# Causal attention on one core: a new order of the steps on each engine, row maxima taken 27 chunks ahead, and their split and the copy of the values on GpSimd

## What is computed

```python
scores = jnp.einsum('bhqd,bhkd->bhqk', Q, K) / np.sqrt(D_HEAD)
causal = jnp.triu(jnp.full((t, t), -jnp.inf, dtype=scores.dtype), k=1)
attn = jax.nn.softmax(scores + causal, axis=-1)
O = jnp.einsum('bhqk,bhkd->bhqd', attn, V)
```

## Time and profile before

| | |
|---|---|
| median of three runs | 861.2 us |
| the profiled execution | 859.2 us, span 857.6 us |
| TensorE busy | 739.3 us, 86% |
| VectorE busy | 683.2 us, 80% |
| ScalarE busy | 567.2 us, 66% |
| GpSimd busy | 423.4 us, 49% |
| attention | 61.5 to 549.8 us |

### The profile page before, as it was taken

The page is one execution under the profiler, slowest core; times in us unless marked ns, Lnnn a source line. Parts: engine busy times, 40 slices in busy tenths (PEclk is TensorE's granted clock), DMA queues, the critical chain, the costliest instruction groups (busy, mean ns, idle before and its releaser), DMA issues. The chain is left out here.

```text
span 857.6 us, 17568 instructions
## 1 busy us (share of the span) xinstructions
PE 739.3 (86%) x4345; PEld 323.0 (38%) x4345; DVE 683.2 (80%) x2289; ACT 567.2 (66%) x926; POOL 423.4 (49%) x468
## 2 busy tenths in 40 slices
PE   6758999999999999999999998696788888887755
PEld 4432233333332333233323331243456555554345
DVE  5669999898988898898889881156788888888883
ACT  4440267666766676667666767558889797897881
POOL 8655112221222112211222122267899999999984
PEclk9875699999999999999999999987999999999997
DMA  6757535335533653364336331201001101100000
GB/s 174 226 152 198 114 71 132 76 93 116 128 76 84 125 120 75 81 137 116 86 74 137 82 68 33 90 2 52 1 0 38 38 1 37 38 1 13 1 14 25
DMA packets 58955, 67.06 MB, mean 78 GB/s; under 512 B 15488, under 2 KB 33536, under 8 KB 58880
## 3 DMA queue, kind: packets, MB, share of 16 engines
q1 hardware_dynamic: 53120, 62.35, 30.5%
q10 hardware_dynamic: 5184, 2.36, 1.0%
q0 software_dynamic: 576, 1.57, 0.7%
HBM read 46.73 MB, written 19.53 MB: 77 GB/s over the span
## 5 line engine op out<-in xcount | busy, mean ns | idle before, releaser
L697 ACT ACTIVATE probs<-ps 128x384 f32<-128x384 f32 (+2 forms) x384 | 291.9, 810 | 174.4 <-PE ps L751 123.4
L668 POOL TENSOR_SCALAR_AFFINE_SELECT probs<-probs 128x256 f32<-128x256 f32 x256 | 102.9, 407 | 368.6 <-ACT probs L697 366.3
L807 DVE CUSTOM_DVE_ANT_0 junk<-ps,tri 128x256 bf16<-128x256 f32 (+3 forms) x512 | 229.1, 488 | 43.7 <-PE ps L719 36.0
L719 PE MATMUL ps<-Kx,Qx 128*128 128x512 bf16 (+3 forms) x768 | 230.8, 345 | 11.3 <-DVE mx L811 4.1
L751 PE MATMUL ps<-Qa,Ka 128*128 128x512 bf16 (+3 forms) x768 | 185.9, 328 | 15.0 <-DMA Qa<-m_scr 10.1
L737 PE MATMUL ps<-probs,Vg 128*9 128x512 f32 (+3 forms) x1536 | 159.3, 488 | 1.0 <-ACT Os L682 0.5
L811 DVE TENSOR_REDUCE mx<-ps 128x1 f32<-128x512 f32 x256 | 158.2, 679 | 0.3 <-DVE Vg L794 0.2
L719 PEld LDWEIGHTS ps<-Kx,Qx 128*128 128x128 bf16 x768 | 68.7, 97 | 204.4 <-DVE mx L807 124.8
L966 POOL TENSOR_TENSOR S<-sim 128x1024 f32<-128x1024 f32 x64 | 120.6, 1907 | 12.1 <-DVE A L1218 6.5
L1218 DVE SCALAR_TENSOR_TENSOR A<-S,T,ps 128x511 f32<-128x511 f32 x128 | 90.2, 741 | 11.3 <-ACT ps L1040 10.3
L751 PEld LDWEIGHTS ps<-Qa,Ka 128*128 128x128 bf16 x768 | 61.5, 97 | 90.8 <-ACT probs L697 44.3
(11 more groups left out here) (115 smaller groups left out, 868.5 us busy)
## 6 DMA issues: line engine op xcount, KB each, us to landing
Qx<-q_scr SPq DMA_DIRECT2D x48, 192.0 KB
Kx<-k_scr SPq DMA_DIRECT2D x48, 192.0 KB
Qa<-q_scr SPq DMA_DIRECT2D x48, 192.0 KB
Ka<-k_scr SPq DMA_DIRECT2D x48, 192.0 KB
o_scr<-Os SPq DMA_DIRECT2D x32, 256.0 KB, 2.1
q_scr<-qs SPq DMA_DIRECT2D x34, 128.0 KB, 3.3
k_scr<-qs SPq DMA_DIRECT2D x18, 128.0 KB, 3.3
xin<-in_L_attn_x_dram ACTq DMA_DIRECT2D x8, 256.0 KB, 3.7
```

Of the source, the lines that this page charges most:

```text
L668: pool.affine_select(out=diag, in_=diag, compare_op=ALU.is_ge, fill=0.0, base=0, pattern=[[0, 2], [1, P]], channel_multiplier=-1).then_inc ...
L697: act.activation(probs[:, k % 2, hh, 0:width], ps[:, bank:bank + 2, :].rearrange("p a c -> p (a c)")[:, 0:width], ACT.Exp, scale=SM_SCALE) ...
L719: pe.matmul(ps[:, X_BANK + f % X_SLOTS, 0:c1 - c0], Qx[:, u, hh, P * i:P * (i + 1)], Kx[:, u, hh, c0:c1], start=True, stop=True).then_inc( ...
L807: dve.tensor_tensor_reduce(out=junk[:, f % 4, 0:w], in0=src, in1=tri[:, CHUNK - w:CHUNK], scale=1.0, scalar=-BIG, op0=ALU.add, op1=ALU.max ...
```

## The change

1. `AHEAD` goes from 20 to 27, and `GROUP_ORDER` has a new order of the same 48 x, 24 s and 12 p.
2. The split leaves VectorE except for its first step (`row_max`) and the turn (`turn_max`), which now comes four chunks later (`TURN_LATER`). In between GpSimd does five steps: the three arithmetic ones, the cast, and a negation of its own into a new tile `mneg`.
3. The copy of the values into `Vg` goes from VectorE to GpSimd.
4. On GpSimd both stand between the masks of unit 1 and those of unit 4.
5. In SyncE's queue the store of an output's second half goes behind the next group's loads of `Qa` and `Ka`, and the store of the first half goes behind the maxima's write and loads.

```diff
-AHEAD = 20
+AHEAD = 27
+TURN_LATER = 4
-GROUP_ORDER = "psxxxpxxsxxsxsxpxspxxsxxpxxxspxxssxxsxpxsxxxsxpxxxsxspsxxsxpxxsxsxxsxpxxsxpxsxsxsxsx"
+GROUP_ORDER = "pxxpsxxsxxxsxxspxpsxsxxpxsxxpxsxsxxsxxxspxsxpxsxsxpxsxxsxpxxsxsxpxsxxsxpxsxsxxsxsxx"
...
                         load_parts(sp, Qa[:, 1 - u], Ka[:, 1 - u], bass.ds(n + 1, 1), sop_loaded[1 - u])
-                        store_o(n, 0)
+                        if not isinstance(n, int) or n > 0:
+                            store_o(n - 1, 1)
                         if ahead:
                             load_next_max(n + 3, 1 - u)
                         m_rows(n + 1, 1 - u, bass.ds(n + 1, 1))
-                        store_o(n, 1)
+                        store_o(n, 0)
...
+                    def split_max(g):
+
+                        c = M_STEPS * g
+                        wait_alone(pool, m_chain, c + 1, pads_made)
+                        pool.tensor_scalar(mneg[:], mm_[:], -1.0, 0.0, ALU.mult, ALU.add)
+                        wait_alone(pool, m_stored, 16 * g, pads_made)
+                        pool.tensor_scalar(msp[:, 0:32], mm_[:], -1.0, 0.0, ALU.mult, ALU.add).then_inc(m_chain, 1)
+                        wait_alone(pool, m_chain, c + 2, pads_made)
+                        pool.tensor_tensor(mr[:], mneg[:], msp[:, 0:32], ALU.subtract).then_inc(m_chain, 1)
+                        wait_alone(pool, m_chain, c + 3, pads_made)
+                        pool.tensor_copy(msp[:, 32:64], mr[:]).then_inc(m_chain, 1)
+                        wait_alone(pool, m_chain, c + 4, pads_made)
+                        pool.tensor_tensor(msp[:, 64:96], mr[:], msp[:, 32:64], ALU.subtract).then_inc(m_chain, 1)
...
+                    def group(n, u, last):
+                        masks(n, DIAG_UNITS[:2])
+                        if not last:
+                            wait_alone(pool, pv_done, PPG * n + PV_START, pads_made)
+                            pool.tensor_copy(Vg[:, 1 - u, :, :, :], vaug[:, bass.ds(n + 1, 1), :, :, :].rearrange(
+                                "p n j h d -> p (n j) h d")).then_inc(v_staged, 1)
+                            split_max(n + 1)
+                        masks(n, DIAG_UNITS[2:])
...
                             if f + AHEAD == CPG - 1 and last < 2:
-                                split_max(n + 1)
+                                row_max(n + 1)
+                            if f + AHEAD == CPG - 1 + TURN_LATER and last < 2:
+                                turn_max(n + 1)
```

More of the change, by code:

```diff
@@ L68 @@
 CPG = len(MAXC)
-AHEAD = 20
-GROUP_ORDER = "psxxxpxxsxxsxsxpxspxxsxxpxxxspxxssxxsxpxsxxxsxpxxxsxspsxxsxpxxsxsxxsxpxxsxpxsxsxsxsx"
+AHEAD = 27
+TURN_LATER = 4
+GROUP_ORDER = "pxxpsxxsxxxsxxspxpsxsxxpxsxxpxsxsxxxsxxxspxsxpxsxsxpxsxxsxpxxsxsxpxsxxsxpxsxsxxsxsxx"
 CARRIED = 4
@@ L576, in build @@
             mm_ = sa("rowmax", [P, 32])
+            mneg = sa("mneg", [P, 32])
             mr = sa("mr", [P, 32])
@@ L626, in group @@
                         m_rows(n + 1, 1 - u, bass.ds(n + 1, 1))
-                        store_o(n, 1)
+                        store_o(n, 0)
                     load_next_max(2, 0)
-                    with sp.Fori(0, GROUPS // 2 - 2) as i:
+                    group(0, 0, True)
+                    group(1, 1, True)
+                    with sp.Fori(1, GROUPS // 2 - 2) as i:
                         for u in range(2):
@@ L635, in _ @@
                     group(GROUPS - 2, 0, False)
+                    store_o(GROUPS - 2, 1)
                     for half in range(2):
@@ L660, in _, with masks @@
                     pool.memset(Ka[:], 1.0).then_inc(pads_made, 1)
-                    def group(n):
-                        for r, k in enumerate(DIAG_UNITS):
+                    def split_max(g):
[10 more added lines that the diff above has]
+                        pool.tensor_tensor(msp[:, 64:96], mr[:], msp[:, 32:64], ALU.subtract).then_inc(m_chain, 1)
+                    def masks(n, units):
+                        for k in units:
                             step = UNITS[k][1][1][3]
@@ L669, in group @@
                                                    pattern=[[0, 2], [1, P]], channel_multiplier=-1).then_inc(masked, 1)
-                    with pool.Fori(0, GROUPS) as n:
-                        group(n)
+                    def group(n, u, last):
[6 more added lines that the diff above has]
+                        masks(n, DIAG_UNITS[2:])
+                    split_max(0)
+                    with pool.Fori(0, GROUPS // 2 - 1) as i:
+                        for u in range(2):
+                            group(2 * i + u, u, False)
+                    group(GROUPS - 2, 0, False)
+                    group(GROUPS - 1, 1, True)
                 @block.scalar
@@ L811, in max_chunk, with row_max @@
                             dve.tensor_reduce(mx[:, hh, i, 0:1], src, AX.X, ALU.max).then_inc(mx_read, 1)
-                    def split_max(g):
-                        c = M_STEPS * g
+                    def row_max(g):
                         dve.wait_ge(mx_read, CPG * (g + 1))
@@ L818, in split_max, with turn_max @@
                                           ALU.max).then_inc(m_chain, 1)
[L819 to L828, removed]
+                        dve.wait_ge(m_chain, M_STEPS * g + 1)
+                    def turn_max(g):
+                        dve.wait_ge(m_chain, M_STEPS * g + M_STEPS - 1)
                         dve.wait_ge(m_stored, 16 * g)
@@ L834, in _ @@
                         max_chunk(0, f)
-                    split_max(0)
+                    row_max(0)
+                    turn_max(0)
                     for f in range(AHEAD):
@@ L840, in group @@
                         for f in range(CPG):
[L841 to L845, removed]
                             if f + AHEAD < CPG and last < 2:
```

## The result

The changed kernel takes 864.2 us, the median of 20 runs (19 of them 859.4 to 872.1), the kernel before 860.7 beside it: 1.0048 times as long, 95% interval 1.0029 to 1.0067. Two single slow runs, one of 1366.1 us of the changed kernel and one of 883.8 us of the kernel before with its loop written out, are left out of the ratios. Forecast were 832 us, in a range of 823 to 847. The profiled execution has a span of 866.2 us.

A forecast was written before the change was run, and what follows sets the result against it. TensorE was to become the bound: floor 26.0 plus 0.6 for exponentials, 26.6 us a group. Attention would end at 522.8, 27.0 before the 549.8; 859.2 − 27.0 = 832 us, range 823 to 847.

The forecast's parts named there:

- The failed step: SyncE's queue: moved output stores go behind DMAs issued within 14 us, their buffers are next used a group later; cost 0.
- the stall: TensorE waiting at each group's first score product for maxima from HBM, 0.8 us a group; forecast to go, slack almost 4.
- group 0: Group without P8 to P11, paced by VectorE: 24 and some waits, 25.0 us, where it took 27.9 before.
- 13 groups without the jump: Groups 1 to 13, paced by TensorE: 26.6 us each, 345.8 in all.
- the 0.6 us for exponentials: Per group, TensorE held by ScalarE's exponentials: 0.25 us at s0.3, 0.25 at s5.2, 0.1 at s2.2.
- two sums, 26.0 and 24.0: Time needed per group: TensorE's floor 26.0 us, VectorE after the change 24.0; so TensorE becomes the bound.
- VectorE's need: VectorE's work per group falls from 25.3 to 24.0 us: 1.0 saved between join and turn, 0.31 by the values' copy.
- GpSimd's steps: Five split steps moved to GpSimd, 0.25 us each plus 0.13 between: 1.9 us, done 2.6 behind the join, cost 0.
- The moved work comes back on VectorE: GpSimd's 2.5 us of steps block VectorE through the shared SBUF port: 27.4 us a group, 843 us; chance 18%.
- The reordering absorbs the exponentials too: The new order of steps hides the exponentials' waits on TensorE: 26.1 us a group, 826 us; chance 12%.
- The maxima still come late: Loads of Qx and the maxima's write land slower at the higher DMA rate, 0.8 us wait remains: 842 us; chance 6%.
- The turn waits for GpSimd: GpSimd steps of 1.02 us hold VectorE's turn 4.0 us: 29.9 a group, 882 us, slower than before; chance 5%.

## Why the prediction was wrong

**The failed step** is one sentence: "The output stores that move on SyncE's queue go behind DMAs that are issued within 14 us, and the next use of their buffers is a group later: cost 0." It counted the stores alone. What they had stood in front of, the six loads of 192 KB, came forward by some 10 us against the first score product, and met VectorE's code: jumps of 3.9 to 5.2 us instead of 2.8 to 2.9, and with the fall of the clock 22.7 us. The reading of the earlier trace rows, "VectorE waits 31.6 us for TensorE, up to 2.3 at a time, behind the stall", missed that in every second group a jump lay inside such a wait. As an account of the time before it holds, since the waits are as long without the jump. But the prediction took away the stall that was the jump's cover, and never had the loop as a step of its own: even with the loads out of the way the jump costs 6 us.

The account of the profiled execution, predicted against measured, for the end of the attention: 522.8 against 557.6.

| term | predicted | measured | difference |
|---|---|---|---|
| first score product | 103.5 | 104.1 | +0.6 |
| group 0 | 25.0 | 27.6 | +2.6 |
| 13 groups without the jump | 26.6 | 27.4 | +10.5 |
| jumps | none | six excesses | +22.7 |
| group 14 | 22.7 | 23.2 | +0.5 |
| group 15 to the end | 25.8 | 23.6 | −2.2 |

These sum to 34.7 of the 34.8; the rest of the kernel takes 308.6 for 307.8 before. Without the jumps it is 844, inside the range, though 12 us from the forecast.

**The second wrong term** is the 0.6 us for exponentials. A group without a jump loses 1.4. TensorE waits for the bank of the chunk three before to be read, at x32, x35, x47 and x23, most behind masked diagonal chunks; of 128 columns VectorE reads one in 0.21 to 0.29 us, and TensorE makes it in a quarter of that or less (128 of the 512 columns that take 0.215). I compared two sums, 26.0 and 24.0, and took the larger; with three banks between the engines, local imbalance costs although either sum fits. The exponentials would cost 0.45 at s0.2, s2.1 and s5.2, near the 0.6, but only once the other waits are gone; which engine TensorE waits for there was not read out. VectorE's need was put at 24.0 us a group; its busy time is 24.5, and 24.4 with the loop written out. The steps that left it were busy for 0.31 + 4 × 0.19 = 1.1 us; the 1.3 in the sum counted the gaps between them as well. One sum is off by a little: 832 + 13 × 0.8 is 842.4, not 843.

**What held.** The stall for the rows goes, and the write follows the join by 203.30 − 200.16 = 3.1, for 3.2 to 3.5 predicted. The runs put the end of the stall down to the queue: with the new queue alone and the loop written out it is gone, so the new order was not needed for it. GpSimd's steps, bounded from other rows, came out at 0.21 to 0.25 each with 0.14 between, and the turn 2.7 behind the join, for 2.6:

```profile
200.16 0.19 DVE L848 TENSOR_TENSOR rowmax<-mx 128x32 f32<-128x32 f32 x1
...
200.51 0.22 POOL L672 TENSOR_SCALAR mneg<-rowmax 128x32 f32<-128x32 f32 x1 [0.47 <-DVE rowmax L848]
...
201.78 0.24 POOL L680 TENSOR_TENSOR msp<-mr,msp 128x32 bf16<-128x32 f32 x1
...
202.87 0.27 DVE L856 STREAM_TRANSPOSE mT<-msp 128x96 bf16<-128x96 bf16 x1
```

VectorE goes on with four chunks meanwhile and does not wait.

**The rivals.** *The moved work comes back on VectorE* fell: without jumps the groups are at its 27.4, but for another reason. With the split back on VectorE they are longer (28.0) and not equal. In the changed kernel with the loop written out the masks still last 407 ns, and VectorE's own instructions last as long as before (422 ns for 256 masked columns in both). The Trainium skill's warning on the shared port (Perfetto Trace Analysis, on optimizing Scalar/DVE operations) does not show here. *The reordering absorbs the exponentials too* fell with the 27.4. *The maxima still come late* fell with the wait gone. *The turn waits for GpSimd* fell, since in the twelve groups the turn waits for nothing; its price of 29.9 a group is near the measured 29.3, which by that number alone would have looked right for a wrong reason. The list had no case of this kind: a transfer that comes earlier and collides.

## What to carry to other kernels

When a queue's order changes, list what is released earlier, not only what is moved, and ask what else uses the DMA engines in the new stretch: code is fetched there too. Idle time named "issue", at equal distances of one loop turn, was here an engine that waited for its own code; look for it in the kernel before, hidden or not, before you take away the wait that hides it. The smallest edit here that beats both kernels is not a reordering of steps: the new queue with VectorE's loop written out takes 848.0 us, with the GpSimd move 844.9, and the new order on top changes nothing that can be told apart (844.2).

## What the runs showed of the hardware

- The jump of VectorE's loop takes 2.8 to 3.1 us from branch to next instruction when the DMA engines are nearly idle (3.2% in the 6 us looked at), and 3.1 to 5.2 beside six loads of 192 KB. In the kernel before, jumps of ScalarE's and GpSimd's loops, once a group, take 0.15 to 0.17 in the attention, and that of TensorE's, which turns once in two groups like VectorE's, 0.27.
- The packets of code on that queue hold 8192 bytes each; the changed kernel has 56 such, 36 with VectorE's loop written out. The second behind a jump starts 3.4 to 3.8 us after it without loads, and at 8.4 to 9.4 us with them. That is when the loads' data end, but for one jump of the kernel before with the new queue, where an output store ran on behind them.
- Behind 3.4 us in which TensorE was busy for 0.61 the granted clock read 0.64 and 0.82 over 6 us; in the run with the later loads, with idle times of 1.2 us and less, it stayed at 1.00.
